# A graph-attention stage whose queries leave the first stage: keys and values only, edge features between the tiles, biases folded

## The chip, the cores and the metric

The kernel runs on one core of a Trainium2 chip. The metric is device time in microseconds, from the program's start to its end, less being better. The engines are TensorE (PE, and PEld for its weight loads), VectorE (DVE), ScalarE (ACT), GpSimd (POOL) and SyncE (SP), which only issues DMAs here.

## The reference

One graph attention layer and one expert layer over N = 6250 nodes of width D = 256, with E = 200000 edges sorted by their target `dst`, 4 heads of 64.

```
h   = layernorm(x)
enh = h + 0.1 * query_emb
Q, K, V = enh @ Wq + bq, enh @ Wk + bk, enh @ Wv + bv      # 4 heads of 64
mod_k  = K[src] + 0.2 * rel_w[edge_type]
scores = sum(Q[dst] * mod_k, -1) / 8
w   = softmax of scores over the edges of one dst
msgs = sum of w * V[src] per dst, or V where a node has no edge
x   = x + layernorm(msgs @ Wo + bo + h) * gamma + beta
x   = x + top-2 of 8 experts (256 -> 1024 gelu -> 256) on layernorm(x)
```

## The kernel before

The program is a sequence of blocks; each block holds one program per engine, and a block ends when all its engines and awaited DMAs have ended. They are: a load of the constants (`build`, L1740), `prepare`, `edge_pass`, a spare pass for unusual inputs that isn't entered, `after_edges`, and `experts`.

`prepare` is the first stage (L521 to L897). Its setup loads the weights and biases (SyncE, L607 to L626) and the edge lists (GpSimd, L649 to L687). VectorE alone makes the edge features from them (L739 to L798), each operation waiting for the one before through `link`. These are `feat` (for each edge, which of 16 rows of a window of nodes it belongs to, and its type), `bases` (the windows' first nodes), a check for unusual inputs, and the lists `keys`, `reach`, `delta` and `penc`. Only then does a loop over NT = 49 tiles of 128 nodes begin. `pipeline` runs every engine's `step`, and `T(k)` is the tile k steps behind. Per tile:

- SyncE loads x into `p_x` (L635), and stores `kept` (x + beta and h + bo, L640) and `kv` (keys and values, L642) of the tile five steps behind. There are R = 4 buffers. x of a tile is issued behind the stores of the tile six before it.
- VectorE takes mean and variance (L805, L819), the reciprocal of the root (L809), normalizes (L824), adds 0.1 query (L832), and evicts keys (L816), values (L827) and queries (L836) from PSUM with their biases.
- ScalarE takes the root (L713) and copies the transposed `enh` (L717) and the transposed queries into `QT` (L720), an SBUF tensor of all 6250 columns.
- TensorE transposes `enh` (L869), multiplies by `wkv` into one bank of 512 columns (L883) and by `wq` (L886), and transposes the queries (L876).
- GpSimd makes `kept` with two sums (L699, L701).

All matmuls are float32, and the trace shows two records for each of them. Last, the 13 tiles of the source lists `ends` are transposed into `idxall` (L841 to L845, L896).

`edge_pass` goes over 261 groups of 6 x 128 edges. GpSimd gathers keys and values of the sources (L240, six per group, U = 6 buffers); it waits for `s_agg`, the end of the sums of the group six before. TensorE's step transposes keys of group g+1 (L432), scores group g (L448 to L456) and sums group g-1 (L467). ScalarE copies `idx` and the window's queries `qb` out of `QT`. VectorE fills some constants at the front of this pass and signals `s_init`.

`after_edges` loads `Wo` and others first (L1215), normalizes and routes; `experts` computes the experts.

Of the kernel before, what the change touches and what calls it, by code (L numbers as in the profile page):

```python
# [8 lines left out]
ACT = mybir.ActivationFunctionType  # L9
# [7 lines left out]
P = 128  # L17
N, D = 6250, 256
H, HD = 4, 64
DC = D // P  # L20
# [117 lines left out]
def edge_pass(nc, ctx, cst, QT, kv_dram, idxall, feat_dram, accs_dram, bases, delta, penc, relT, reach, keys, spots):  # L138
# [60 lines left out]
    s_px = sem("es_px")  # L199

# [6 lines left out]
    with nc.Block() as blk:  # L207
# [39 lines left out]
        def _(act):  # L247
            act.preload_act_table(ACT.Exp)
            act.wait_ge(s_init, 4)

            def step(T):
                n = T(-AHEAD)
                if n.live:

                    if n.first >= U:
                        act.wait_ge(s_kv[n.slot], n.rnd * (16 * TG))
                    act.copy(idx[n.slot][:, :].rearrange("p (c j) -> p c j", c=2),
                             idxall[:, 0:2 * NG * TS].rearrange("p (c q) -> p c q", c=2)[:, :, bass.ds(n.t * TS, TS)]
                             ).then_inc(s_idx, 1)
# [160 lines left out]
        def _(pe):  # L420
            pe.wait_ge(s_init, 4)
# [99 lines left out]
def prepare(nc, ctx, cst, io, out, dram, QT, idxall, bases, delta, penc, relT, unfit, reach, keys):  # L521
# [9 lines left out]
    R = 4  # L531
# [3 lines left out]
    enh = [sb(f"p_enh{i}", [P, D]) for i in range(R)]  # L535
    enhT = [sb(f"p_enhT{i}", [P, DC, P]) for i in range(R)]
    qrow = [sb(f"p_q{i}", [P, D]) for i in range(R)]
# [3 lines left out]
    wq = sb("p_wq", [P, DC, D])  # L541
    bias = sb("p_bias", [P, 5, D])
    qe = sb("p_qe", [P, D])
    qe01 = sb("p_qe01", [P, D])
# [14 lines left out]
    odd = sb("p_odd", [1, 4])  # L559
# [7 lines left out]
    psT = ctx.enter_context(nc.psum_tensor("p_psT", [P, 512], F32))  # L567
    psKV = [ctx.enter_context(nc.psum_tensor(f"p_psKV{i}", [P, 512], F32)) for i in range(2)]
    psQ = [ctx.enter_context(nc.psum_tensor(f"p_psQ{i}", [P, 512], F32)) for i in range(2)]
    psQT = ctx.enter_context(nc.psum_tensor("p_psQT", [P, 512], F32))  # L570
    psI = ctx.enter_context(nc.psum_tensor("p_psI", [P, 2, 512], F32))
    ident = cst("ident")

    s_w = sem("ps_w")
# [13 lines left out]
    s_bn = sem("ps_bn")  # L588
    s_ln = sem("ps_ln")
    s_xb = sem("ps_xb")  # L590
    s_sd = sem("ps_sd")
    s_eT = sem("ps_eT")
    s_qT = sem("ps_qT")
    s_ev = sem("ps_ev")
    s_t = sem("ps_t")
    s_mm = sem("ps_mm")
    s_tq = sem("ps_tq")

    MF = 2 * len(chunks)
    SET0 = 8  # L600
    SET1 = SET0 + 14 * len(chunks) + 7
    SET2 = SET1 + 18
    rowof = [0, NG * TS, 2 * NG * TS]

    with nc.Block() as blk:
        @blk.sync
        def _(sp):  # L607
            for a in range(DC):
                rowsl = slice(a * P, (a + 1) * P)
                sp.dma_start(wkv[:, a, 0:D], io["Wk"][rowsl, :]).then_inc(s_w, 16)  # L610
                sp.dma_start(wkv[:, a, D:2 * D], io["Wv"][rowsl, :]).then_inc(s_w, 16)
                sp.dma_start(wq[:, a, :], io["Wq"][rowsl, :]).then_inc(s_w, 16)
            for j, name in enumerate(("bq", "bk", "bv", "bo", "beta")):
                sp.dma_start(bias[:, j, :], io[name].rearrange("(a d) -> a d", a=1).to_broadcast([P, D])
                             ).then_inc(s_w, 16)
            sp.dma_start(qe[:, :], io["query"].rearrange("(a d) -> a d", a=1).to_broadcast([P, D])
                         ).then_inc(s_w, 16)
# [10 lines left out]
            def step(T):  # L628
                g = T(0)
                if g.live:  # L630
                    r0 = node_rows(g.t)
                    if g.first >= R:
                        hold(sp, s_ln, (g.t - R) * 3 + 2)
                        hold(sp, s_xb, (g.t - R) * 2 + 1)
                    sp.dma_start(xin[g.slot][:, :], io["x"][bass.ds(r0, P), :]).then_inc(s_x[g.slot], 16)  # L635
                o = T(5)
                if o.live:
                    lo, r = own_rows(o.t)
                    hold(sp, s_xb, o.t * 2 + 2)
                    sp.dma_start(dram["kept"][r, :], kept[o.slot][lo:P, :]).then_inc(s_st[o.slot], 16)  # L640
                    hold(sp, s_ev, o.t * 3 + 3)
                    sp.dma_start(dram["kv"][r, :], kvrow[o.slot][lo:P, :]).then_inc(s_st[o.slot], 16)  # L642
            pipeline(sp, NT, 0, 5, R, 2 * R, step)
# [6 lines left out]
        def _(pool):  # L650
# [6 lines left out]
            pool.dma_start(seq[0:GE, 0:E // GE], io["dst"].rearrange("(p e) -> p e", p=GE)).then_inc(s_seq, 16)  # L657
# [30 lines left out]
            for c, (g0, n) in enumerate(chunks):  # L688

                pool.wait_ge(s_set, SET0 + 14 * (c + 1))  # L690
                for a in range(2):
                    pool.dma_start(dram["feat"][a, g0:g0 + n], feat[c][0:n, a]).then_inc(s_f, 16)

            def step(T):
                g = T(0)
                pool.wait_ge(s_x[g.slot], (g.rnd + 1) * 16)
                if g.first >= R:
                    pool.wait_ge(s_st[g.slot], g.rnd * 32)
                pool.tensor_tensor(kept[g.slot][:, D:2 * D], xin[g.slot][:, :], bias[:, 4, :], ALU.add).then_inc(s_xb, 1)  # L699
                pool.wait_ge(s_ln, g.t * 3 + 2)  # L700
                pool.tensor_tensor(kept[g.slot][:, 0:D], xn[g.slot][:, :], bias[:, 3, :], ALU.add).then_inc(s_xb, 1)  # L701
            pool.wait_ge(s_w, 16 * 18)
            pipeline(pool, NT, 0, 0, R, R, step)

        @blk.scalar
        def _(act):
            act.preload_act_table(ACT.Sqrt)

            def step(T):
                g, e, q = T(0), T(2), T(5)  # L710
                if g.live:
                    act.wait_ge(s_bn, g.t * 2 + 2)
                    act.activation(stat[g.slot][:, 8:9], stat[g.slot][:, 7:8], ACT.Sqrt, bias=cst("eps")  # L713
                                   ).then_inc(s_sd, 1)
                if e.live:
                    act.wait_ge(s_t, e.t + 1)
                    act.copy(enhT[e.slot][:, :, :].rearrange("p a q -> p (a q)"), psT[:, 0:D]).then_inc(s_eT, 1)  # L717
                if q.live:
                    act.wait_ge(s_tq, q.t + 1)
# [1072 lines left out]
```

## Time and profile before

| what | us |
|---|---|
| time, median of 3 runs | 3416.37 (3415.4 to 3417.13) |
| the profiled execution | 3421.45 |
| its span, first to last instruction | 3419.6 |
| TensorE busy in the span | 2775.5 (81%) |
| GpSimd busy | 2020.8 (59%) |
| VectorE busy | 1676.3 (49%) |
| ScalarE busy | 1281.9 (37%) |

Shares of the whole span average over stages with different limits: the table is to be read beside the stages, whose borders in the trace are 231.9 (end of `prepare`), about 2238 (end of `edge_pass`) and about 2742 (`experts` begins).

### The profile page before, as it was taken

How to read it: one execution, taken by the hardware profiler on the slowest of the kernel's cores; microseconds unless marked ns; L12 is line 12 of the kernel's file. 1: busy time of each engine (PE TensorE's matmuls, PEld its weight loads, DVE VectorE, ACT ScalarE, POOL GpSimd, SP SyncE). 2: the span in 40 equal slices, each digit the busy share in tenths (PEclk: the TensorE clock that was granted, in tenths of full speed). 3: DMA queues.
4: the chain of work that ended last, by engine and by line, in shares of the span. 5: the costliest groups of instructions: out<-in, count | busy, mean ns of one | idle time of the engine just before them, and what ended most of it. 6: DMA issues, size and time to landing. Idle time of an engine off the chain costs nothing. (4 is left out here: it accounts for less than half of the span.)

```text
span 3419.6 us, 74395 instructions
## 1 busy us (share of the span) xinstructions
PE 2775.5 (81%) x19652; PEld 1892.4 (55%) x19652; DVE 1676.3 (49%) x6055; ACT 1281.9 (37%) x4194; POOL 2020.8 (59%) x2106
## 2 busy tenths in 40 slices
PE   2977878887788878888888878866555999999998
PEld 1644444444444444444444444544444888888887
DVE  5756555555555555555555555577671111111111
ACT  0224444444444444444444444423342222222222
POOL 3547777777777777777777777667762222222222
PEclk9989999999999899999999999955557999999999
DMA  4658888888888888888888888755436666666664
GB/s 112 215 192 237 240 244 244 237 243 244 243 240 243 242 244 241 240 243 244 239 241 244 244 242 236 227 162 155 151 123 207 185 184 184 184 184 184 184 184 101
DMA packets 337412, 721.17 MB, mean 211 GB/s; under 512 B 43947, under 2 KB 184226, under 8 KB 337217
## 3 DMA queue, kind: packets, MB, share of 16 engines
q0 software_dynamic: 152560, 456.14, 48.4%
q1 hardware_dynamic: 184784, 264.35, 24.9%
q14 instruction: 52, 0.42, 0.0%
q8 instruction: 16, 0.26, 0.0%
HBM read 639.58 MB, written 80.74 MB: 211 GB/s over the span
## 5 line engine op out<-in xcount | busy, mean ns | idle before, releaser
L240 POOL DMA_INDIRECT e_kv<-d_kv,e_idx x1566 | 1503.8, 960 | 496.8 <-issue 451.7
L432 PE MATMUL psK<-consts,e_kv 128*128 128x128 f32 x3132 | 545.6, 301 | 234.7 <-DMA e_kv<-d_kv,e_idx 233.9
L432 PEld LDWEIGHTS psK<-consts,e_kv 128*128 128x128 f32 x3132 | 354.5, 148 | 378.8 <-issue 319.4
L1615 POOL DMA_INDIRECT out<-f_y,f_whose x112 | 174.0, 1553 | 648.5 <-DVE f_y L1668 634.7
L1634 ACT ACTIVATE f_hT<-f_psH,f_b 128x256 f32<-128x256 f32 x448 | 212.5, 474 | 590.1 <-PE f_psH L1712 590.0
L1712 PE MATMUL f_psH<-f_xT,f_w 128*128 128x256 f32 x1792 | 398.2, 381 | 1.4 <-DVE f_xT L1654 1.4
L1702 PE MATMUL f_psY<-f_w,f_hT 128*128 128x256 f32 x1792 | 396.0, 379 | 0.0
L326 DVE COPY e_kT<-psK 128x384 f32<-128x384 f32 x522 | 287.8, 551 | 198.6 <-PE psK L432 197.5
L1712 PEld LDWEIGHTS f_psH<-f_xT,f_w 128*128 128x128 f32 x1792 | 342.0, 191 | 48.6 <-DMA f_w<-in_W 1.7
L1702 PEld LDWEIGHTS f_psY<-f_w,f_hT 128*128 128x128 f32 x1792 | 336.2, 190 | 43.4
L268 ACT COPY e_qb<-QT 64x32 f32 x1044 | 229.4, 220 | 307.8 <-issue 288.5
L467 PE MATMUL psA<-e_kv,e_probT 128*32 128x128 f32 x6264 | 337.9, 289 | 0.4 <-ACT e_probT L306 0.4
L285 ACT ACTIVATE e_carried<-psA,e_small 128x130 f32<-128x130 f32 x261 | 96.7, 370 | 622.3 <-PE psA L467 622.3
L363 DVE TENSOR_TENSOR e_accs<-psA,e_carried 128x128 f32<-128x128 f32 x261 | 76.4, 293 | 474.1 <-ACT e_carried L285 474.1
L274 ACT COPY e_kT<-psK 128x384 f32<-128x384 f32 x522 | 248.7, 476 | 130.2 <-PE psK L432 124.7
L456 PE MATMUL psD<-e_kT,e_qb 128*32 128x384 f32 x2088 | 253.4, 561 | 0.0
L505 PE MATMUL psP<-consts,e_prob 128*128 128x128 f32 x783 | 142.8, 291 | 123.3 <-ACT e_prob L294 123.3
L1654 DVE TENSOR_SCALAR f_xT<-f_psT,f_ln 128x256 f32<-128x256 f32 x112 | 55.8, 540 | 378.3 <-PE f_psT L1690 378.3
L351 DVE TENSOR_REDUCE e_small<-psD 128x1 f32<-128x384 f32 x261 | 145.0, 556 | 128.0 <-PE psD L456 124.6
L467 PEld LDWEIGHTS psA<-e_kv,e_probT 128*32 128x32 f32 x6264 | 124.9, 109 | 124.2 <-issue 95.5
L478 PEld LDWEIGHTS psA<-e_accs,e_carry 128*128 128x128 f32 x522 | 84.4, 203 | 190.5 <-issue 189.9
L1665 DVE TENSOR_TENSOR f_yb<-f_psY,f_b 128x256 f32<-128x256 f32 x112 | 47.6, 425 | 269.5 <-PE f_psY L1702 269.5
(238 smaller groups left out, 4176.2 us busy)
## 6 DMA issues: line engine op xcount, KB each, us to landing
f_w<-in_W SPq DMA_DIRECT2D x112, 1024.0 KB, 8.0
e_rows<-d_feat SPq DMA_DIRECT2D x174, 288.0 KB
e_kv<-d_kv,e_idx POOLq DMA_INDIRECT x1566
d_accs<-e_accs SPq DMA_DIRECT2D x87, 195.0 KB
f_xs<-d_xs SPq DMA_DIRECT2D x56, 258.0 KB, 2.8
n_kept<-d_kept SPq DMA_DIRECT2D x49, 256.0 KB, 3.4
d_kept<-p_kept SPq DMA_DIRECT2D x48, 256.0 KB, 2.2
d_kv<-p_kv SPq DMA_DIRECT2D x48, 256.0 KB, 2.0
```

What stands on the lines that cost most here:

```text
L240: pool.indirect_dma_start(out=kv[g.slot][:, t, :], out_offset=None, in_=kv_dram[:, :], in_offset=bass.IndirectOffsetOnAxis(ap=idx[g.slot][ ...
L268: act.copy(qb[a.slot % R][o * HD:(o + 1) * HD, :].rearrange("p (c b w o) -> p c b w o", c=2, b=DC, o=2)[:, c, :, :, o], QT[o * HD:(o + 1) ...
L274: act.copy(kT[a.slot % 2][:, 1, j * GH:(j + 1) * GH], psK[:, 1, 0:GH]).then_inc(s_kTa, 1)
L326: dve.tensor_copy(kT[a.slot % 2][:, 0, j * GH:(j + 1) * GH], psK[:, 0, 0:GH]).then_inc(s_kTv, 1)
L351: dve.tensor_reduce(sm[:, MX], psD[:, g.slot % 2, 0:GH], AX.X, ALU.max).then_inc(s_m, 1)
L432: mm = pe.transpose(psK[:, half, t * P:(t + 1) * P], kv[a.slot][:, third * TS + t, half * P:(half + 1) * P], ident)
L456: mm = pe.matmul(psD[own, g.slot % 2, 0:GH], qb[g.slot % R][:, own], kT[g.slot % 2][:, b, c * GH:(c + 1) * GH], start=False, stop=True, ti ...
L467: mm = pe.matmul(psA[own, 0:2 * HD], probT[c.slot % R][:, j, own], kv[c.slot][:, s * TS + j, D + b * P:D + (b + 1) * P], start=j == 0, sto ...
L1615: pool.indirect_dma_start(out=out[:, :], out_offset=bass.IndirectOffsetOnAxis(ap=whose[c.slot][:, a:a + 1], axis=0), in_=y[c.slot][:, a, : ...
L1634: act.activation(hT[:, c, :], psH[:, c % 4, 0:BT], ACT.Gelu, bias=b1[:, bass.ds(e * FC + c, 1)]).then_inc(s_g, 1)
L1702: mm = pe.matmul(psY[:, t, 0:D], hT[:, f, t * P:(t + 1) * P], w2[c.slot][:, f, :], start=f == 0, stop=f == FC - 1)
L1712: mm = pe.matmul(psH[:, f % 4, 0:BT], w1[g.slot][:, a, f * P:(f + 1) * P], xT[g.slot][:, a, :], start=a == 0, stop=a == DC - 1)
```

## The change

- The block that loads the constants goes; `prepare` loads them behind the first x tile and each engine waits for what it needs. R becomes 6. SyncE's order of loads is new: x 0, constants, Wk, Wv, x 1, query (by columns), bk, x 2 and 3, Wq, Wo, bv and bq (by columns), bo, beta, x 4 and 5, the relations, bases, mid, and the 781 KB of dst (`seq`, before on GpSimd). The last 13 of them are `SMALL`. `feat` is stored by SyncE at step 47 instead of by GpSimd.
- The tile's x is normalized by ScalarE (a scale and a bias per row) instead of VectorE. The sum with 0.1 query is gone: `0.1 query @ Wk + bk` is computed once as `biask` and added at the keys' eviction, `0.1 query @ Wv + bv` goes through Wo into `biaso` (the weights of a node's edges sum to 1), which takes bo's place in `kept`, and values are copied by ScalarE without a bias.
- TensorE multiplies keys and values alone, in two banks, and no queries. The transposed normalized x is copied straight into `QT`.
- The edge features are cut by `yield` into some 86 pieces, one or two of which VectorE does in each of 53 steps. All loops are written out instead of looped in hardware.
- `edge_pass` begins with the queries: 13 chunks of 512 columns, computed in place from `QT`, evicted by ScalarE with the bias `bqc`. ScalarE copies the first six `idx` ahead of them.
- `Wo` stays in SBUF from `prepare` to `after_edges`.

```
 # edge_pass
+            for t in range(U):
+                listed(t, t)
+
+            for i, q in enumerate(QCH):
+                act.wait_ge(s_q, i + 1)
+                for b in range(DC):
+                    act.activation(QT[:, b, q], psQ[i % 2][:, b, 0:q.stop - q.start], ACT.Identity,
+                                   bias=bqc[:, b:b + 1]).then_inc(s_qe, 1)
+            act.wait_ge(s_qe, DC * len(QCH))
             act.wait_ge(s_init, 4)
...
         @blk.tensor
         def _(pe):
+            for i, q in enumerate(QCH):
+                if i >= 2:
+                    pe.wait_ge(s_qe, DC * (i - 1))
+                for b in range(DC):
+                    for a in range(DC):
+                        mm = pe.matmul(psQ[i % 2][:, b, 0:q.stop - q.start], wq[:, a, b * P:(b + 1) * P], QT[:, a, q],
+                                       start=a == 0, stop=a == DC - 1)
+                mm.then_inc(s_q, 1)
+            pe.wait_ge(s_qe, DC * len(QCH))
             pe.wait_ge(s_init, 4)
...
 # prepare, SyncE
+            for s in range(R, NT + 5):
+                if s < NT:
+                    hold(sp, s_xn, s - R + 1)
+                    hold(sp, s_k1, s - R + 1)
+                    load(s)
+                if s == NT - 2:
+
+                    hold(sp, s_set, N_FEAT)
+                    for c, (g0, n) in enumerate(chunks):
+                        for a in range(2):
+                            sp.dma_start(dram["feat"][a, g0:g0 + n], feat[c][0:n, a]).then_inc(s_f, 16)
+                for o in (range(s - 4) if s == R else (s - 5,)):
+                    lo, r = own_rows(o)
+                    hold(sp, s_evv, o + 1)
+                    hold(sp, s_ek, o + 1)
+                    sp.dma_start(dram["kv"][r, :], kvrow[o % R][lo:P, :]).then_inc(s_st[o % R], 16)
+                    hold(sp, s_k0, o + 1)
+                    sp.dma_start(dram["kept"][r, :], kept[o % R][lo:P, :]).then_inc(s_st[o % R], 16)
...
 # prepare, GpSimd
+            pool.wait_ge(s_w, SMALL)
+            for g in range(NT):
+                i = g % R
+                pool.wait_ge(s_x[i], (g // R + 1) * 16)
+                if g >= R:
+                    pool.wait_ge(s_st[i], (g // R) * 32)
+                pool.tensor_tensor(kept[i][:, D:2 * D], xin[i][:, :], rowsof[:, BETA, :], ALU.add).then_inc(s_k1, 1)
+                if g == 0:
+                    pool.wait_ge(s_set, N_BO)
+                pool.wait_ge(s_xn, g + 1)
+                pool.tensor_tensor(kept[i][:, 0:D], xn[i][:, :], biaso[:, :], ALU.add).then_inc(s_k0, 1)
...
 # prepare, ScalarE
+            for s in range(NT + 4):
+                g, f, m, c = s, s - 1, s - 2, s - 4
+                if 0 <= m < NT:
+                    act.wait_ge(s_t, m + 1)
...
+                    act.copy(QT[:, :, bass.ds(node_rows(m), P)],
+                             psT[m % 2][:, 0:D].rearrange("p (a q) -> p a q", a=DC)).then_inc(s_eT, 1)
+                if 0 <= c < NT:
+                    act.wait_ge(s_mm, c + 1)
...
+                    act.copy(kvrow[c % R][:, D:2 * D], psKV[1][c % 2][:, 0:D]).then_inc(s_evv, 1)
+                if 0 <= f < NT:
...
+                    act.activation(xn[f % R][:, :], xin[f % R][:, :], ACT.Identity, bias=stat[f % R][:, 10:11],
+                                   scale=stat[f % R][:, 9:10]).then_inc(s_xn, 1)
+                if g < NT:
+                    act.wait_ge(s_bn, g * 2 + 2)
+                    act.activation(stat[g % R][:, 8:9], stat[g % R][:, 7:8], ACT.Sqrt, bias=cst("eps")
                                    ).then_inc(s_sd, 1)
...
 # prepare, VectorE
+            extra = setup()
+            for s in range(NT + 4):
+                g, f, c = s, s - 1, s - 4
...
+                    dve.bn_stats(stat[g % R][:, 0:6], xin[g % R][:, :]).then_inc(s_bn, 1)
+                if 0 <= f < NT:
+                    dve.wait_ge(s_sd, f + 1)
+                    dve.reciprocal(stat[f % R][:, 9:10], stat[f % R][:, 8:9]).then_inc(s_ln, 1)
+                if g < NT:
+                    hold(dve, s_bn, g * 2 + 1)
+                    dve.bn_aggr(stat[g % R][:, 6:8], stat[g % R][:, 0:6]).then_inc(s_bn, 1)
+                if 0 <= f < NT:
+                    dve.wait_ge(s_ln, f * 2 + 1)
+                    dve.tensor_scalar(stat[f % R][:, 10:11], stat[f % R][:, 6:7], stat[f % R][:, 9:10], -1.0,
+                                      ALU.mult, ALU.mult).then_inc(s_ln, 1)
+                next(extra, None)
+                if 0 <= c < NT:
+                    dve.wait_ge(s_mm, c + 1)
+                    if c >= R:
+                        dve.wait_ge(s_st[c % R], (c // R) * 32)
+                    dve.tensor_tensor(kvrow[c % R][:, 0:D], psKV[0][c % 2][:, 0:D], biask[:, :], ALU.add
+                                      ).then_inc(s_ek, 1)
+                    next(extra, None)
...
 # prepare, TensorE: step s transposes tile s - 2 and multiplies tile s - 3
+            for s in range(2, NT + 3):
+                m, k = s - 2, s - 3
+                if s == AT_COLS:
+                    pe.wait_ge(s_w, SMALL)
...
+                if 0 <= k < NT:
+                    pe.wait_ge(s_eT, k + 1)
...
+                    for j in range(2):
+                        mm = into(psKV[j][k % 2][:, 0:D], lambda a: QT[:, a, bass.ds(node_rows(k), P)],
+                                  lambda a: wkv[:, a, j * D:(j + 1) * D])
                     mm.then_inc(s_mm, 1)
```

The small products of TensorE stand at its steps 3 (`AT_COLS`), 6 (`AT_BO`), 30, 32 and, for the index lists, 36 to 42.

## Rows read from the trace of the kernel before

**Rows 1.** Windows: stretch, length, busy PE, PEld, DVE, ACT, POOL, granted clock, DMA share, GB/s

```profile
0.00:30.30 30.30, 0.00 (x0) 0.00 (x0) 0.54 (x4) 1.30 (x2) 14.45 (x30) 1.00 0.87 218
30.30:65.90 35.60, 2.77 (x8) 1.53 (x8) 30.42 (x75) 0.00 (x0) 3.90 (x7) 1.00 0.06 23
65.90:221.90 156.00, 151.20 (x586) 94.58 (x586) 117.96 (x393) 40.79 (x146) 75.67 (x97) 1.00 0.57 200
221.90:231.90 10.00, 2.46 (x15) 1.61 (x15) 3.16 (x6) 0.38 (x1) 0.00 (x0) 0.84 0.11 42
```

**Rows 2.** Line L240, GpSimd's gathers: ns min/median/max, first and last start

```profile
L240 POOL DMA_INDIRECT e_kv<-d_kv,e_idx x1566: 949/953/1483, 234.5 to 2214.4; - x196
```

**Rows 3.** Timeline, two steps of the edge pass, TensorE: start, us, what

```profile
279.86 0.85 PE L432 MATMUL psK<-consts,e_kv 128*128 128x128 f32 x6
...
284.15 0.43 PE L467 MATMUL psA<-e_kv,e_probT 128*32 128x128 f32 x8
...
286.14 0.85 PE L432 MATMUL psK<-consts,e_kv 128*128 128x128 f32 x6
```

**Rows 4.** Timeline, TensorE in one tile of the first stage

```profile
142.38 0.38 PE L869 MATMUL p_psT<-consts,p_enh 128*128 128x128 f32 x2
...
142.81 1.88 PE L883 MATMUL p_psKV<-p_wkv,p_enhT 128*128 128x512 f32 x4
144.53 1.03 PE L886 MATMUL p_psQ<-p_wq,p_enhT 128*128 128x256 f32 x4
145.40 0.38 PE L869 MATMUL p_psT<-consts,p_enh 128*128 128x128 f32 x2
```

**Rows 5.** Waits between 80 and 210: total us, times, longest

```profile
DVE p_stat L805 <- DMA p_x<-in_x: 14.0, 22, 2.3
DVE p_kv L816 <- PE p_psQ L886: 13.1, 29, 0.8
```

**Rows 6.** Timeline, SyncE at the start

```profile
0.72 0.40 SPq L1740 DMA_DIRECT2D consts<-in_consts  x1
4.37 0.34 SPq L610 DMA_DIRECT2D p_wkv<-in_Wk  x1
```

**Rows 7.** Timeline, first tiles, VectorE and TensorE

```profile
69.82 0.42 DVE L805 BATCH_NORM_STATS2 p_stat<-p_x 128x6 f32<-128x256 f32 x1
...
70.44 3.62 PE L883 MATMUL p_psKV<-p_wkv,p_enhT 128*128 128x512 f32 x4
70.44 0.88 DVE L824 TENSOR_SCALAR p_xn<-p_x,p_stat 128x256 f32<-128x256 f32 x1
```

**Rows 8.** Timeline, first tiles, SyncE and VectorE

```profile
77.81 0.34 SPq L642 DMA_DIRECT2D d_kv<-p_kv  x1
...
78.30 0.34 SPq L635 DMA_DIRECT2D p_x<-in_x  x1
...
80.62 0.43 DVE L805 BATCH_NORM_STATS2 p_stat<-p_x 128x6 f32<-128x256 f32 x1 [0.51 <-DMA p_x<-in_x]
```

**Rows 9.** Timeline of a steady tile, VectorE, then SyncE

```profile
142.06 0.43 DVE L805 BATCH_NORM_STATS2 p_stat<-p_x 128x6 f32<-128x256 f32 x1 [0.68 <-DMA p_x<-in_x]
...
143.97 0.42 DVE L836 TENSOR_TENSOR p_q<-p_psQ,p_bias 128x256 f32<-128x256 f32 x1
...
147.77 0.43 DVE L805 BATCH_NORM_STATS2 p_stat<-p_x 128x6 f32<-128x256 f32 x1 [0.35 <-DMA p_x<-in_x]
...
144.52 0.33 SPq L642 DMA_DIRECT2D d_kv<-p_kv  x1
145.67 0.35 SPq L635 DMA_DIRECT2D p_x<-in_x  x1
```

**Rows 10.** Timeline, VectorE in the setup

```profile
55.36 1.83 DVE L781 TENSOR_TENSOR p_drop<-p_seq 125x1600 f32<-125x1600 int32 x1
```

**Rows 11.** Timeline, SyncE at the end of the stage

```profile
222.02 0.24 SPq L642 DMA_DIRECT2D d_kv<-p_kv  x1
```

**Rows 12.** Tile p_enh, VectorE: ns min/median/max

```profile
L832 DVE TENSOR_TENSOR p_enh<-p_xn,p_qe x49: 409/417/946, 67.6 to 213.0; 128x256 f32<-128x256 f32 x49
```

More of the change, by code:

```diff
@@ L199, in edge_pass @@
     s_px = sem("es_px")
+    s_q = sem("es_q")
+    s_qe = sem("es_qe")
+    QCH = [slice(q, min(q + 512, N)) for q in range(0, N, 512)]
+    psQ = (psD, psK)
     LO, HI, WARM = -1, 2, 8
@@ L252, in step @@
                 n = T(-AHEAD)
[L253 to L259, printed above, removed]
+                if n.live and n.first >= U:
+                    act.wait_ge(s_kv[n.slot], n.rnd * (16 * TG))
+                    listed(n.t, n.slot)
                 a = T(-1)
@@ L518, in own_rows, with prepare @@
     return lo, bass.ds(node_rows(t) + lo, P - lo)
[L521 removed]
+def prepare(nc, ctx, cst, io, out, dram, QT, idxall, bases, delta, penc, relT, unfit, reach, keys, wq, wo, bqc, consts):
     def sb(name, shape, dt=F32):
@@ L626, in _ @@
                                                                                ).to_broadcast([P, 1])).then_inc(s_w, 16)
[L628 to L643, printed above, removed]
+            sp.dma_start(seq[0:GE, 0:E // GE], io["dst"].rearrange("(p e) -> p e", p=GE)).then_inc(s_w, 16)
+            for s in range(R, NT + 5):
[15 more added lines that the diff above has]
+                    sp.dma_start(dram["kept"][r, :], kept[o % R][lo:P, :]).then_inc(s_st[o % R], 16)
             for i in range(R):
@@ L838, in _, with broadcast @@
-            pipeline(dve, NT, 0, 4, R, 2 * R, step)
-            dve.wait_ge(s_src, 16 * 5)
-            dve.tensor_copy(endsf[:, :, :], ends[:, :, :]).then_inc(s_back, 1)
-            for i, c in enumerate(range(0, IT, 4)):
-                n = min(IT - c, 4)
-                dve.wait_ge(s_turn, i + 1)
-                dve.tensor_copy(idxall[:, c * P:(c + n) * P], psI[:, i % 2, 0:n * P]).then_inc(s_back, 1)
+            def broadcast(which, col):
+                for a in range(DC):
+                    link(dve.tensor_scalar(spread[:, which, a, :], cst("ones"), cols[:, col, a:a + 1], None, ALU.mult))
@@ L847, in _ @@
+            for _ in extra:
+                pass
         @blk.tensor
         def _(pe):
-            pe.wait_ge(s_w, 16 * 18)
-            for b in range(2):
-                mm = pe.transpose(psQT[:, b * NREL:(b + 1) * NREL], relraw[:, :], ident[0:NREL, 0:NREL])
-            mm.then_inc(s_pb, 1)
-            pe.wait_ge(s_set, SET1)
-            for a, ps in enumerate((psT, psKV[1])):
-                pe.matmul(ps[:, 0:NG], cst("ones")[0:1, :], basef[0:1, a, :], start=True, stop=True).then_inc(s_pb, 1)
@@ L857, in _, with into @@
-            pe.wait_ge(s_set, SET1 + 4)
-            pe.matmul(psKV[0][0:1, 0:1], misfits[:, 0:1], cst("ones")[:, 0:1], start=True, stop=True
-                      ).then_inc(s_pb, 1)
-            pe.wait_ge(s_set, SET1 + 14)
-            def step(T):
-                g, m, c = T(2), T(3), T(5)
-                if g.live:
-                    pe.wait_ge(s_ln, g.t * 3 + 3)
-                    if g.first >= 1:
-                        pe.wait_ge(s_eT, g.t)
+            def into(ps, lhs, rhs):
+                for a in range(DC):
+                    mm = pe.matmul(ps, lhs(a), rhs(a), start=a == 0, stop=a == DC - 1)
+                return mm
```

427 lines of the change are left out of this document (235 added, 192 removed).

## The prediction

> **What bounds the kernel now.** I read the table of stages first [rows 1]. The whole first stage ends at 231.9; the edge pass runs from there to about 2215 and the rest needs no more than a glance, since the change leaves it as it is. In the edge pass GpSimd's gathers are the bound: 1566 of them start between 234.5 and 2214.4, one per 1.265 us, six per group, 7.59 us per group [rows 2]. TensorE needs less: a step with all its data present takes 286.14 - 279.86 = 6.28 us [rows 3]. So a microsecond saved before 231.9 is kept in full, provided that the gathers are not held up later.
>
> Before 231.9 there are four stretches [rows 1]. To 30.3 the engines wait for the first loads. From 30.3 to 65.9 VectorE computes the edge features alone (30.4 us busy in 35.6) and TensorE does nearly nothing. From 65.9 to 221.9 come the 49 node tiles. From 221.9 to 231.9 almost nothing computes.
>
> In the tile stretch TensorE is full: a tile is 3.02 us from transpose to transpose, of which the key/value matmuls take 144.53 - 142.81 = 1.72, the query ones 145.40 - 144.53 = 0.87, and two pairs of transposes 142.81 - 142.38 = 0.43 [rows 4]. The waits show a second bound just under it: VectorE waited 14.0 us for x tiles and 13.1 for TensorE [rows 5]. The reader should keep that in mind: the load of tile o+6 is behind the stores of tile o in SyncE's program, and x arrives late 22 times already.
>
> **The change, part by part.**
>
> *Start.* The block that waited for the constants goes. SyncE's first ordinary load was issued at 4.37 after a start at 0.72, and the wait for all 18 loads ended at 30.3 with the DMA queues full (share 0.87 of the stretch) [rows 1, 6]. The new kernel must still have almost the same bytes before its second tile: four broadcast vectors of 128 KB go, Wo (256 KB), two more x tiles (256 KB) and the 4-byte column loads come, and the 781 KB copy of dst moves to the end of SyncE's queue, which `SMALL` waits for. TensorE waits for `SMALL` ahead of tile 1, GpSimd ahead of its first tile. I take 30.3 - 3.7 for the earlier start, + 3 for bytes and small packets now in front: 29.5, bounds 26 and 33.
>
> *Fill.* Behind that wait TensorE has 8 one-column products and then slow matmuls: the first four key/value records took 3.62 us instead of 1.88 [rows 4, 7]. Tile 0 is done at about 36, tiles 1 and 2 at 38 and 40, then the small products for `biaso`, GpSimd's first sum at 42.5 and the next at 44. `kept` of tiles 0 and 1 must be issued before x of tile 7, so VectorE's step 7 starts at about 44.6 + 2.3 = 47.
>
> *A tile.* TensorE loses the queries and one pair of transposes: 3.02 - 0.87 - 0.22 = 1.93 us. Moving keys and values into separate matmuls of 256 columns costs nothing by the query ones, whose four records of that width take 0.87. ScalarE has a copy of 0.37, one of 0.35, the new normalization (about 0.38, the size of VectorE's) and a root of 0.29: 1.4 us, no bound. GpSimd's two sums stay at 1.6. What binds is the loop through SyncE: key eviction of tile o ends; SyncE issues kv(o), kept(o), x(o+6), 0.49 apart [rows 8]; x arrives 80.62 - 78.30 = 2.3 after its issue [rows 8], and I take 2.5 because 512 KB of stores now stand right ahead of it; then VectorE goes from bn_stats to the operation behind bn_aggr in 0.62 [rows 7], does the small product (0.1 to its issue), one piece of edge work, and evicts the keys of tile o+2, 0.42 for a tile of this form [rows 9]. That is two tiles per 0.1 + 0.98 + 2.5 + 1.14 = 4.7 us plus the piece: 2.3 to 2.4 us a tile bare, 2.55 with a piece of 0.5. The same sum for the old order: from the end of the eviction (143.97 + 0.42) to the kv store 0.13, to the load 145.67 - 144.52 = 1.15, to bn_stats 147.77 - 145.67 = 2.1, through VectorE's old step 143.97 + 0.42 - 142.06 = 2.33 [rows 9]: 5.7, or 2.85 a tile. That is just under TensorE's 3.02, as the waits had it [rows 5], so the loop is real.
>
> *Edge features.* Their work is 30.4 us of the setup [rows 1], plus the index turning (2.2, and a cast of 1.0), plus about 3 for the folded biases. Counting the generator's pieces against the steps, steps 7 to 26 hold about 1.0 us each. VectorE's own chain is 1.14 with the eviction, so 2.2, which fits under 2.55. Steps 27 to 30 hold 2.0, 2.4, 2.6 and 2.9 (the 1.83 us comparison over dst [rows 10], the reduction of the same size, the cast of the lists, the scan): with 1.14 each, 14 us. Steps 31 to 48 have little: 18 x 2.3 = 41.4. Steps 49 to 52 load nothing: 4 x 1.93 = 7.7. The six `feat` stores, formerly issued by GpSimd in idle time, now stand in SyncE's program ahead of the last tiles: 2.5 us of issue and 0.8 MB of queue, 3 us. The four index turnings add 1.5. Sum: 47 + 20 x 2.55 + 14 + 41.4 + 7.7 + 4.5 = 165.6.
>
> *Tail.* Before, the last `kv` store was issued at 222.02 [rows 11] and the stage let go at 231.9, while DMA was busy at a share of 0.11 and moved 42 GB/s [rows 1]: the two last stores, of 106 partitions and 212 KB each, crawl. Both stay, now issued together, so 10.7 us where it was 9.9. Stage end: 176.5, against 231.9: **55.4 earlier**.
>
> *Queries in the edge pass.* TensorE now computes 13 chunks of 4 matmuls before its first group. Per column that is what a tile's queries cost: 0.87 x 6250/128 = 42.5 us, plus about 2.5 for a start at the low clock (the granted clock is down to 0.84 over the stretch ahead [rows 1], and low it costs 3.62 against 1.88 for the same records [rows 4, 7]) and for the last eviction: 45. The evictions, 26 on ScalarE of about 0.6, hide under it. Then come a filling step of 3.7, one without sums of 4.9, and the sums of group 0 at 284.15 + 0.43 - 279.86 = 4.7 into the third step [rows 3]: 13.3. Group 0 is done 58.3 after the stage boundary. GpSimd has six buffers: it starts 2.6 in (234.5 against 231.9) and has issued 36 gathers at 2.6 + 45.5 = 48.1 [rows 2]. It then stands until 58.3: **10.2 us lost**, once. The backlog goes away because a step of 6.28 beats 7.59. What is queued behind GpSimd's wait is only further gathers. Moving the index copies ahead of `s_init` gives 0.3 back.
>
> *Wo's loads* leave the third stage. GpSimd's gathers bound the beginning there as well: I count nothing, and it could only add to the gain.
>
> **Sum.** -55.4 + 10.2 - 0.3 = -45.5. The profiled execution took 3421.45 us (span 3419.6, 1.9 around it), which is 5.1 above the median of 3416.37. I put the difference on the median: 3371.
>
> **A rule weighed.** The edge work now runs beside GpSimd's sums. One VectorE operation with two SBUF inputs already varies from 0.409 to 0.946 us beside them, with a median of 0.417 [rows 12]. The Trainium skill, page "SBUF — State Buffer", section "SBUF: two separate sides", says that VectorE (in its two-port modes, or with two SBUF inputs) and GpSimd take a shared port pair exclusively, for a whole instruction. The trace agrees for this operation; nothing here shows it for the integer casts. By the spread of the row, 0.946 - 0.417 = 0.5 for an operation that meets a sum: nothing if the pieces fall between the sums, as the median has it, 20 steps x 2 pieces x 0.5 = 20 us if all meet one. I count nothing in the sum, since 2.2 has 0.35 of slack under 2.55; the other end is rival 2.
>
> **Rivals.**
> 1. *TensorE binds after all* (x arrives in time, because chains of different parity overlap or the queue is quick): steps of 1.93 after the edge work, 2.2 (VectorE) within it. 47 + 44 + 14 + 35 + 8 + 3 = 151, stage end 162, -70 + 10 = -60: 3356. For it: VectorE waited for x only 22 of 43 times [rows 5]. Against it: the loop sum, which comes out at 2.85 where the waits show it near 3.02. Chance 0.17.
> 2. *VectorE binds* through the port and x comes later still behind the stores, 3.0 us in the first twenty steps and 2.7 after: +9 +7, and with pieces that meet GpSimd in steps 27 to 30, +3: about -26: 3390. Chance 0.20.
> 3. *The gathers lose far more than 10 us*: if a backlogged step took 7.6 instead of 6.28, the backlog would never shrink, but the loss would stay at what is lost at first; if on top TensorE stayed at its low clock (records of twice the length [rows 4, 7]) through all the queries, group 0 is done at 87 + 13 + 8 = 108 and 60 us are lost: -55 + 60 = +5: 3421. It turns slower once the queries take over 90 us. Against it: in the tile stretch the long records of the beginning [rows 7] had become the short ones [rows 4] with nothing but matmuls back to back, and the queries are just that. Chance 0.03.
> 4. *The change gives nearly nothing early*: the loads in front, with 4-byte columns, reach beyond 45 us. Chance 0.03, about 3390 at the worst, which the range takes in.
>
> **Chances and range.** Forecast (3371, its own range 3362 to 3382) 0.57, the rivals as above. The range 3353 to 3395 reaches over rivals 1 and 2. A measurement of this kernel tells about 0.2%, 7 us, from no change: faster 0.95, same 0.02, slower 0.03.
>
> **What would show it.** Right: p_x still the wait ahead of bn_stats, a tile of 2.3 to 2.6 us with TensorE idle 0.4 or more in each; the stage boundary near 176; one wait of GpSimd for psA of about 10 us and then none; 42 to 46 us of query matmuls. A boundary near 162 shows rival 1; tiles of 3 us with VectorE busy throughout, rival 2; matmul records of double length all through the queries, rival 3. The prediction is wrong if steps with edge work leave VectorE without idle time, or if GpSimd waits for psA in many groups.

## The result, and the profile after

The changed kernel takes 3378.0 us (median of 4 runs, 3376.1 to 3380.7), the kernel before 3415.9 beside it: ratio 0.989, 95% interval 0.987 to 0.991, so 37.9 us less. The forecast was 3371, within 3353 to 3395. The profiled execution took 3379.7 us, against 3421.45 before.

The table of stages of the changed kernel (columns as in [rows 1]):

```profile
30.10:48.10 18.00, 17.04 (x72) 14.09 (x72) 5.11 (x25) 5.78 (x17) 5.53 (x9) 1.00 0.23 85
48.10:172.50 124.40, 100.45 (x457) 76.38 (x457) 81.88 (x290) 61.39 (x173) 66.59 (x91) 0.97 0.72 240
172.50:184.60 12.10, 0.00 (x0) 0.00 (x0) 0.00 (x0) 0.00 (x0) 0.00 (x0) 0.57 0.20 71
```

TensorE, with 151.2 busy in 156 us the bound of the tile stretch before [rows 1], now stands idle for 24 of 124 us. The stage lets go at 184.6, where it was 231.9: 47.3 us earlier.

Timeline of the changed kernel, VectorE in two consecutive steps, then SyncE's loads and stores of the same time (idle before and releaser in brackets):

```profile
55.86 0.43 DVE L921 BATCH_NORM_STATS2 p_stat<-p_x 128x6 f32<-128x256 f32 x1
...
56.98 0.42 DVE L937 TENSOR_TENSOR p_kv<-p_psK,p_biask 128x256 f32<-128x256 f32 x1
57.32 0.35 DVE L856 CAST p_feat<-p_type 128x384 bf16<-128x384 int32 x1
60.52 0.43 DVE L921 BATCH_NORM_STATS2 p_stat<-p_x 128x6 f32<-128x256 f32 x1 [2.86 <-issue]
```

```profile
55.45 0.33 SPq L686 DMA_DIRECT2D d_kv<-p_kv  x1
55.91 0.35 SPq L688 DMA_DIRECT2D d_kept<-p_kept  x1
56.43 1.87 SPq L639 DMA_DIRECT2D p_x<-in_x  x1
58.88 0.34 SPq L686 DMA_DIRECT2D d_kv<-p_kv  x1
```

The order kv, kept, x is the loop of the prediction: a load is issued about 1 us behind the eviction that the kv store waits for, and VectorE's step two tiles later waits for its landing. Here one load took 1.87 us to issue instead of 0.34, and VectorE stood for 2.86. Between 48 and 172.5 VectorE stood three times for such a load (issues of 1.87, 0.87 and 1.69; 7.0 us together) and 15 times, 21.1 us, for x otherwise.

The waits between 48 and 172.5 of the changed kernel (total us, times, longest); the second row answers to the first of [rows 5]:

```profile
ACT p_xn L767 <- DVE p_stat L930: 39.6, 33, 3.2
DVE p_stat L921 <- DMA p_x<-in_x: 21.1, 15, 3.4
DVE p_stat L921 <- issue: 7.0, 3, 2.9
```

Behind the boundary, the gathers of the changed kernel, as [rows 2], and then GpSimd's waits between 150 and 260:

```profile
L244 POOL DMA_INDIRECT e_kv<-d_kv,e_idx x1566: 949/953/1467, 187.0 to 2179.4; - x196
```

```profile
POOL e_kv L244 <- ACT e_idx L254: 19.5, 1, 19.5
...
POOL e_kv L244 <- PE psA L491: 12.4, 1, 12.4
```

The gathers start 47.5 us earlier and end 35.0 earlier. What lies between is the one stall of 12.4 us for the sums of group 0; every later wait for them is 0.3. The first gather of the next stage (`n_agg`) starts 34.0 earlier, 2204.3 against 2238.3, and the end of the span comes 41.7 earlier. So 7.7 us more were gained behind the gathers, in code whose only edit is that Wo is no longer loaded there.

### The profile page after: what moved, and what is told of

Same layout as the page of the kernel before. It is cut to its first block and busy times, and to the rows that moved or that the text cites. A ratio compares the mean times of both kernels' runs of the same rounds, so it can differ in the third digit from the quotient of the medians.

```text
span 3377.9 us, 73501 instructions
## 1 busy us (share of the span) xinstructions
PE 2780.7 (82%) x19682; PEld 1902.6 (56%) x19682; DVE 1612.8 (48%) x5916; ACT 1327.4 (39%) x4269; POOL 2014.1 (60%) x2099
## 5 line engine op out<-in xcount | busy, mean ns | idle before, releaser
L529 PEld LDWEIGHTS psP<-consts,e_prob 128*128 128x128 f32 x783 | 80.8, 140 | 176.3 <-ACT e_prob L309 176.3
```

The costliest lines, as they stand in the source:

```text
L529: mm = pe.transpose(psP[:, j * P:(j + 1) * P], prob[g.slot % R][:, j * P:(j + 1) * P], ident)
```

## The experiments

All are made from the changed kernel, where nothing else is said. The boundary is where the query matmuls start (L441). The kernel before was run again beside each group of runs, with medians of 3415.9 to 3419.3 (3415.9 beside the changed kernel, 3419.0 beside the first four runs below), so a difference between two groups is uncertain by some 3 us; ratios are to the kernel before in the same group. Positions within a run come from one profiled execution each, and they vary too: the last eviction ends at 172.5, 175.0, 172.1 and 172.2 in the changed kernel and in the next three whose tiles are the same (stores split, one chunk, features by GpSimd).

**Stores a step later.** The loop's own test: the load of tile s is issued ahead of the stores of tile s-6 instead of s-5.

```diff
-            for s in range(R, NT + 5):
+            for s in range(R, NT + 6):
-                for o in (range(s - 4) if s == R else (s - 5,)):
+                for o in (s - 6,):
```

> Change: SyncE queues a tile's two stores one step later, so that the load of tile s goes ahead of the stores of tile s-6 instead of s-5; nothing else. Theory (the loop of x behind the stores, with the landing of x and the eviction of an older tile in it, sets the period of about 2.4 us): the load no longer waits on the previous tile's eviction, the normal period falls to what TensorE or VectorE need, 2.0 to 2.2 us, and the boundary after the first stage comes at 160 to 175 us instead of 184.6; total 3354 to 3369. Rival A (VectorE or TensorE is the bound, and the waits for x are only its shadow): period and boundary within 2 us of now, total 3376 to 3380. Rival B (the DMA engines, busy 0.72 here, are the bound): no change either, with the landing of x longer than 2.3 us.

Measured: 3358.5 us (3354.5 to 3359.4), 19.5 less than the changed kernel; ratio to before 0.9823 (0.9807 to 0.9839). The boundary comes at 163.8, 20.8 earlier. The loop now runs over three tiles instead of two, since a load waits for an eviction one tile older. Its stages, and its wait for x between 48 and 151.5:

```profile
48.10:151.50 103.40, 94.18 (x451) 73.71 (x449) 80.08 (x277) 59.20 (x169) 65.86 (x88) 1.00 0.84 283
151.50:163.80 12.30, 0.01 (x1) 0.04 (x1) 0.06 (x1) 0.05 (x2) 0.00 (x0) 0.62 0.21 73
```

```profile
DVE p_stat L921 <- DMA p_x<-in_x: 8.2, 8, 3.3
```

The same work is done in 103.4 us instead of 124.4, with TensorE busy 91% of it. Both rivals fall: neither TensorE nor VectorE nor the DMA engines (share 0.84 now, 0.72 then) were the bound. The place of two stores in SyncE's program was.

**The last stores split.** The last tile's two stores of 106 partitions become four, of 96 and 10 partitions.

```diff
+                    parts = [own_rows(o)] if o < NT - 1 else [
+                        (P - 96, bass.ds(N - 96, 96)), (NT * P - N, bass.ds(LAST + NT * P - N, N - (NT - 1) * P - 96))]
...
-                    sp.dma_start(dram["kv"][r, :], kvrow[o % R][lo:P, :]).then_inc(s_st[o % R], 16)
+                    for (lo, r), n in zip(parts, size):
+                        sp.dma_start(dram["kv"][r, :], kvrow[o % R][lo:lo + n, :]).then_inc(s_st[o % R], 16)
... (kept likewise; the wait at the end counts two stores more)
```

> Change: the last tile's two stores, of 106 partitions each, are made as 96 and 10 partitions each; nothing else. Theory (the 12.1 us between the last eviction and the boundary are the last stores landing slowly for their 106 partitions, 71 GB/s in that window against 240 before): the tail falls to 3 to 5 us, the total by 7 to 9 us to 3369 to 3371. Rival (the tail is the queue's remaining stores, or the end of the block itself): no change, 3376 to 3380.

Measured: 3370.3 us (3369.0 to 3372.4), 7.8 less; ratio 0.9855 (0.9839 to 0.9872). The last eviction ends at 175.0 and the boundary is at 179.0: a tail of 4.0 instead of 12.1. (The boundary is 5.6 earlier and not 8, since the tiles of this execution ended 2.5 later, with the same code.) The window of that tail:

```profile
175.00:179.00 4.00, 0.00 (x0) 0.00 (x0) 0.00 (x0) 0.00 (x0) 0.00 (x0) 0.72 0.64 219
```

In the changed kernel, of 40 slices between 165 and 186 the last stores' read

```profile
DMA  0898997000089999511111111111111111100005
GB/s 0 316 382 300 332 379 289 0 0 0 0 304 386 378 386 371 180 12 16 8 39 47 55 47 55 51 51 51 51 55 47 55 47 55 47 35 0 0 0 93
```

The stores crawl at mostly 47 to 55 GB/s, with between one and two tenths of the DMA engines busy; split, the same bytes move at 219 in the window above. The Trainium skill, page "DMA: Bandwidth & Descriptors", section "Why a DMA increments its semaphore by 16 and not by 1", says that a DMA uses the largest number of engines up to 16 that divides the outer dimension: 2 for 106, 16 for 96, 10 for 10. The trace agrees for 106 partitions (2 of 16 is 0.125). For the split stores it shows a share of 0.64 over the tail, far more than 2 engines, but not which store had how many.

**One chunk of queries.** The price of the moved queries; the run leaves out 12 of the 13 chunks.

```diff
-    QCH = [slice(q, min(q + 512, N)) for q in range(0, N, 512)]
+    QCH = [slice(q, min(q + 512, N)) for q in range(0, N, 512)][:1]
```

> Leaves out 12 of the 13 chunks of queries (the output is then not the reference's). Theory (the 45 us of queries lie beside the gathers' latency and the fill, and only the stall of GpSimd, 12.1 us by its longest wait, is on the path): the total falls by 11 to 14 us, to 3364 to 3367. Rival (the query work adds to the end in full, 41 us of the 45): the total falls to about 3337. Second rival (GpSimd's gathers catch up on their own): no fall.

Measured: 3366.6 us (3363.7 to 3367.8), 11.4 less, ratio 0.9844 (0.9827 to 0.9860), with the boundary at 184.4, as good as unmoved. GpSimd's wait for group 0's sums:

```profile
POOL e_kv L244 <- PE psA L491: 0.6, 2, 0.3
```

The 12 chunks left out are some 41 of the 44 us of query work; the time falls by about the stall of 12.4 alone.

**Edge features stored by GpSimd.**

```diff
-                            sp.dma_start(dram["feat"][a, g0:g0 + n], feat[c][0:n, a]).then_inc(s_f, 16)
+                if g == NT - 11:
+                    pool.wait_ge(s_set, N_FEAT)
+                    (the same six stores as pool.dma_start)
```

> Change: the six stores of edge features are issued by GpSimd after its tile 42 instead of by SyncE ahead of its stores of tile 46. Theory (they hold SyncE and the DMA engines while tile 48's load waits: a wait of 3.4 us at 160 us): boundary 2 to 4 us earlier, total 3374 to 3376. Rival (the last tiles wait for the stores ahead of them in any case, or GpSimd's issuing stalls kept rows): no change or 1 to 3 us slower.

Measured: 3377.0 us (3375.9 to 3380.1), ratio 0.9878 (0.9861 to 0.9894), boundary 184.5. That is 1.0 us less than the changed kernel, or 3.8 by the ratios, whose intervals overlap; that isn't separated from no change. In the profile the last load of x is issued at 160.4 instead of 161.2 and the last eviction starts 0.3 earlier (171.8 against 172.1). So the profile shows 0.1 to 0.7 us for the six stores on SyncE, where the prediction had 3, and the expected 2 to 4 us did not come; the times can't exclude them.

**The kernel before with stores a step later.**

```diff
-                o = T(5)
+                o = T(6)
... (the loop runs one step longer)
```

> The kernel before with the one edit of the run that moved the stores a step later: SyncE queues the stores of tile s-6 at step s instead of s-5. Theory (before, TensorE with 2.97 us a tile in steady state sets the pace, and the loop of load behind stores came into being with the change): no measurable change, ratio 0.998 to 1.002. Rival (the loop held the kernel before as well): 10 to 20 us faster. Its profile also says how far the stages after the first differ between two profiled executions of the kernel before: from the first n_agg to the end it took 1181.3 us; if that was the run, 1173 to 1177 now; if the change made those stages shorter, 1181 again.

Measured: ratio 1.0001 (0.9992 to 1.0010), 10 runs against 15. The edit that is worth 19.5 us in the changed kernel is worth nothing in the one before. Its trace says why. Between 80 and 210 VectorE no longer waits for x at all (14.0 us before, [rows 5]), and waits for TensorE instead, which is busy in 130.0 of the 130 us (129.5 before):

```profile
DVE p_kv L816 <- PE p_psQ L886: 29.7, 43, 1.1
```

Its profile also says what the two kernels differ in behind the gathers. From first `n_agg` to the end it took 1178.9 us, which lies in neither of the ranges expected. With the profiles of all runs of this section the picture is clear all the same: 1178.7 to 1181.6 in the four of before and its variants, 1171.7 to 1174.3 in the ten of the changed kernel and those made from it. Some 2.5 us vary from run to run; the rest, 4 us or more, is a property of the programs.

**Both edge pieces behind the eviction.**

```diff
-                next(extra, None)
+                if c < 0:
+                    next(extra, None)
                 if 0 <= c < NT:
                     ...
                                       ).then_inc(s_ek, 1)
                     next(extra, None)
+                    next(extra, None)
```

> The changed kernel, with both edge pieces of a step on VectorE behind the eviction of the keys (as it is, one lies between a tile's statistics and the eviction, one behind it). Same work, same stores. Theory (the loop runs from an eviction over SyncE and the load of x to the statistics and the next eviction but one; a piece ahead of the eviction lies in it, a piece behind it lies in the wait for x): with 0.3 to 0.4 us a piece, 0.15 to 0.2 us less per tile over some 40 tiles, total 4 to 8 us less, 3370 to 3374. Rival (VectorE's sum of work sets the period, wherever it stands in the step): no change, 3376 to 3380.

Measured: 3372.5 us (3369.8 to 3376.7), 5.5 less, ratio 0.9872 (0.9857 to 0.9887), whose interval overlaps the changed kernel's (0.9872 to 0.9907), so the time alone doesn't show a gain. The boundary tells more: 178.7, 5.9 earlier, where the same tiles varied by 3 in the four profiles named above. VectorE does the same work, but the piece now lies in the wait for x. Between 48 and 166.5 that wait, against 21.1 us and 15 times in the changed kernel, is

```profile
DVE p_stat L921 <- DMA p_x<-in_x: 27.1, 23, 3.5
```

VectorE waits longer and the kernel is faster. Its load isn't the bound; its order was a part of the loop.

**Both edits that paid.**

> The changed kernel with both edits that paid: stores a step later (measured -19.6 us alone) and the last tile's stores split into 96 and 10 partitions (-7.8 alone). Theory (one acts on the tiles, the other on the tail, so they add): 3349 to 3352. Rival (with the tiles closer together the last stores queue at the DMA engines, busy 0.85, and the tail grows again): 3354 to 3358.

Measured: 3349.6 us (3348.0 to 3352.0), ratio 0.9801 (0.9787 to 0.9814); last eviction 152.5, boundary 156.5, tail 4.0. They add: 19.5 + 7.8 = 27.3 expected, 28.4 measured, with the 3 us of uncertainty between groups.

**And the edge pieces behind the eviction as well.**

> As the run before, and with both edge pieces behind the eviction. Theory (with the stores a step later the load of x no longer waits for the eviction, TensorE is busy 94% of the steady stretch and sets the period, so where the pieces stand no longer matters): within 2 us of the run before. Rival (VectorE's order still sets the period): 3 to 6 us faster than it.

Measured: 3351.3 us (3344.5 to 3352.2), ratio 0.9799 (0.9786 to 0.9813). The boundary is at 154.1, 2.4 earlier, but the time is the same within the spread. In the profiles the gathers start 2.5 earlier, the stall for the sums of group 0 is 13.8 instead of 12.4, and the last gather starts only 0.3 earlier. Of the 5.5 us nothing that can be measured is left once the load waits for an eviction one tile older.

**The gap at VectorE's loop turn, three runs.** They ran on another chip, on which the kernel before takes 4006 us and the gathers end some 570 us later (below); the stage in question lasts as long there as before. The first two are the kernel before with

```diff
+            for _ in range(64):      # 24 in the second
+                dve.nop(nofuse=True)
```

> The kernel before with 64 instructions that do nothing on VectorE, at its start, where it waits for its loads until 40 us. Question: in the stage behind the gathers VectorE stands idle with nothing shown as its cause, before tile 26, 33 and 40 of 49 (where its loop of seven tiles turns), 21.2 and 19.6 us in two profiles of the kernel before and 11.7 to 13.9 us in all eight profiles of kernels made from the changed one. Theory (the gap depends on where the loop's code lies in VectorE's program, which the change moved): with the code moved by 64 instructions the gaps change, to 10 to 30 us, and the stage from first n_agg to first f_psT, 363.3 to 364.8 us before, with them; total 3410 to 3425. Rival (something the change did there, its one edit being that Wo is no longer loaded in it): 19 to 22 us and 363 to 365 us as they were.

> The same with 24 such instructions. Theory (place of the code): gaps of VectorE at the turn of the loop other than 19 to 22 us in this run or in the one with 64. Rival (Wo's loads, or data): 19 to 22 us in both.

> The changed kernel with Wo's two loads issued again at the start of the stage behind the gathers, and waited for there, as in the kernel before; nothing else. Theory (place of VectorE's code): gaps of VectorE at the loop's turns stay at 11 to 14 us, the stage from the first n_agg to the first f_psT at 356 to 357 us or up to 1 us more for the loads; total 3376 to 3380. Rival (those loads are what made the stage 7 us longer in the kernel before): 362 to 365 us, total 3383 to 3387.

Measured: ratios to before 1.0000 (0.9990 to 1.0010), 1.0002 (0.9992 to 1.0012) and 0.9913 (0.9897 to 0.9930). VectorE's idle time with no cause shown, in front of `n_y`: first the two profiled executions of before and after on the first chips, then 64 instructions more, 24 more, and the changed kernel with Wo's loads back:

```profile
DVE n_y L1364 <- issue: 21.2, 5, 7.0
```

```profile
DVE n_y L1469 <- issue: 13.0, 8, 4.1
```

```profile
DVE n_y L1366 <- issue: 21.1, 5, 6.9
```

```profile
DVE n_y L1366 <- issue: 19.3, 5, 6.6
```

```profile
DVE n_y L1470 <- issue: 13.0, 8, 4.3
```

The stage from first `n_agg` to first `f_psT` took 364.9, 362.9 and 357.5 us, against 364.8 and 356.6 in the two kernels. The loads of Wo account for 0.9 us of the 8.2 at most (357.5 against 356.6), and moving VectorE's code by 24 or 64 instructions left the gaps as they were. Neither theory explains the gap; the last section has what the traces show beside it.

**A chunk of queries in the tail.** From the kernel with both edits that paid: nodes 0 to 511 are projected behind the last tile, in the PSUM tiles of the transposes.

```diff
-    QCH = [slice(q, min(q + 512, N)) for q in range(0, N, 512)]
+    QCH = [slice(q, min(q + 512, N)) for q in range(512, N, 512)]
+            pe.wait_ge(s_eT, NT)
+            for b in range(DC):
+                mm = into(psT[b][:, 0:512], lambda a: wq[:, a, b * P:(b + 1) * P], lambda a: QT[:, a, 0:512])
+            mm.then_inc(s_mm, 1)
... (ScalarE evicts both halves into QT with bqc and waits for that)
```

> The kernel with stores a step later and the last stores split, and the first chunk of queries (nodes 0 to 511) made at the end of the first stage, behind the last tile's values, while the last stores land; 12 chunks stay beside the gathers. Theory (the tail of 4 us leaves TensorE idle, and the stall of GpSimd, 12 us, shrinks by what the queries end earlier): the chunk's 3.5 us are hidden in the tail, the boundary stays within 1 us, the stall falls by 3 to 4 us, total 3345 to 3347, ratio to before 0.979. Rival (the chunk, with its eviction, ends after the stores have landed and holds the boundary by what it saves): no change against the run without it, 3349.6, ratio 0.980.

Measured: 3346.7 us (3344.9 to 3351.3), ratio 0.9792 (0.9778 to 0.9805). The boundary is at 159.3, 4.7 behind the last eviction (154.6) where it was 4.0 (156.5 and 152.5). It is 2.8 later, not within 1 us as expected, 2.1 of it from tiles that the edit doesn't touch. The stall

```profile
POOL e_kv L244 <- PE psA L491: 7.3, 1, 7.3
```

was 12.4; it fell by 5.1, more than the expected 3 to 4. In the profile the gathers, first to last, take 1985.6 instead of 1992.3. By the medians it is 2.9 us faster than the run without it, with overlapping intervals: the stall is shorter, the gain of the whole isn't shown beyond the spread.

## Why the prediction was right

In the profiled executions the sum reads: boundary -47.3 (forecast -55.4), the first gather behind it -0.2 (forecast -0.3), gathers from first to last +12.5 (forecast +10.2 of stall), the step from the last gather to `n_agg` +1.0, behind it -7.7 (forecast 0). Together -41.7, forecast -45.5. By the medians it is -37.9, as measured beside the changed kernel, and with before's 3417.5 of the later 15 runs -39.5; before's profiled execution was slower than its median, as the prediction had it.

*Start and fill: right, within about 1 us.* TensorE came out of its wait at 30.1 (29.5), VectorE's step 7 started at 48.1 (47).

*The mechanism of the tile: right, and shown.* The experiment on the stores took the loop away and with it 21 us of the stage; the pieces moved behind the eviction took 5.9, close to half a piece a tile; and before, where TensorE's 3.02 lay above the loop's 2.85, the same edit did nothing. *Its size: too small.* The term that failed is the tile with edge work, 2.55: the 20 steps from 48.1 to 103.6 took 55.5 us, 2.77 each, 4.5 us more than forecast. 1.0 of that is a slip in the prediction's own working, since (4.7 + 0.5) / 2 is 2.6. What was left out are the slow issues of loads: three in these steps, 1.5, 0.5 and 1.4 us longer than 0.34. If they lie in the loop in full they make 3.4 us, the rest; no run removed them alone, so this share is worked out and not shown. TensorE's clock is no part of it: it was granted at 0.50 (1.2 GHz) from 62 to 65 and from 96 to 99, behind idle times of 2.49 and 2.16, as here,

```profile
58.51 1.03 PE L947 MATMUL p_psV<-p_wkv,QT 128*128 128x256 f32 x4
62.02 0.69 PE L994 MATMUL p_psT<-consts,p_xn 128*128 128x128 f32 x2 [2.49 <-ACT p_xn L767]
62.50 1.91 PE L947 MATMUL p_psK<-p_wkv,QT 128*128 128x256 f32 x4
```

but VectorE's eviction waited for TensorE in none of these steps, only for the last three tiles (5.2 us). ScalarE's normalization also takes 0.60, not the 0.38 taken from VectorE's, but lies in no loop that bound:

```profile
L767 ACT ACTIVATE p_xn<-p_x,p_stat x49: 599/600/612, 17.4 to 166.1; 128x256 f32<-128x256 f32 x49
```

Steps 27 to 30 took 13.8 (14), the rest 55.2 (53.6). The last eviction ended at 172.5, not 165.6. (With a tail of 10.7 the prediction's stage end is 176.3, not the 176.5 that it went on with.)

*The tail: 12.1, not 10.7*, and with the right cause, 106 partitions. *The queries: 44 (45), slow start included.* The granted clock was 0.50 (1.2 GHz) from 184.6 to 186, behind 12 us in which TensorE did nothing, and a record there took 1.19 us instead of 0.59. For the slow records of [rows 7], which the prediction put down to the same low clock, the trace doesn't show it: the granted clock reads 1.00 from 70 to 78. *The stall: 12.4, not 10.2*, since group 0 was done 59.8 behind the boundary, not 58.3, and the gathers were ready 0.6 sooner.

*Rival 1* (3356, boundary 162) is what the changed kernel becomes with the stores a step later: 163.8 and 3358. *Rival 2*, VectorE as the bound through the port (3390), is the nearest in time beside the forecast, since 3378 lies between the two, but not its mechanism: with the stores a step later the same VectorE work fits into 103 us instead of 124. The subtraction over the edges, with one SBUF tensor as input, stayed near its shortest time beside GpSimd's sums:

```profile
L842 DVE TENSOR_SCALAR p_epos<-p_epos,p_start x6: 768/785/869, 52.4 to 95.3; 128x384 f32<-128x384 f32 x4, 5x384 f32<-5x384 f32 x2
```

An operation with two SBUF inputs did meet a sum at 107.8. It was the sum that lasted longer there, 1.81 us instead of the usual 0.73, and not VectorE's operation (1.82; 1.83 in [rows 10]).

*Rivals 3 and 4* are out by the same rows: 44 us of queries, one stall of 12.4, and TensorE out of its wait at 30.1.

*Wo's loads* were counted at nothing. Putting them back cost at most 1 us, so that stands. The 7.7 us that the stage behind the gathers gained were foreseen by nothing, and they made good most of what the tiles lacked: the right total owes as much to that as to the sum. That part is luck. Without it the time would have been near 3386, still within 3353 to 3395 but outside the forecast's own 3362 to 3382, and nearer to rival 2's 3390 than to 3371.

## What to carry to other kernels

When one engine's work per tile is cut, write out the loop that runs through the queue of loads and stores, from an eviction over the store that waits for it and the load queued behind that store to the next tile but one: it can be the next bound, and one more step between a load and the stores ahead of it may stretch it out of the way (here half of what the change itself gave, and nothing in the kernel where TensorE was the bound). Look at the number of partitions of a stage's last stores: with 106 they took 12 us to land, as 96 and 10 they took 4. Work moved beside a latency still shows as far as it delays the first result for which a full set of buffers waits.

## What the runs showed of the hardware that was not expected

- *VectorE stands idle where its loop of seven tiles turns.* In the changed kernel, where the eviction of tile 26 is ready to go:

```profile
2361.60 0.18 DVE L1444 BATCH_NORM_AGGREGATE n_st<-n_st 128x2 f32<-128x6 f32 x1
2364.89 0.42 DVE L1469 TENSOR_TENSOR n_y<-n_psO,n_kept 128x256 f32<-128x256 f32 x1 [3.12 <-issue]
```

and in the kernel before, the same two instructions:

```profile
2395.02 0.18 DVE L1339 BATCH_NORM_AGGREGATE n_st<-n_st 128x2 f32<-128x6 f32 x1
2402.17 0.42 DVE L1364 TENSOR_TENSOR n_y<-n_psO,n_kept 128x256 f32<-128x256 f32 x1 [6.96 <-issue]
```

  In the profile a packet of 8 KB on the queue called instruction falls into these gaps, and into none of VectorE's other pauses of over 1.5 us in this loop. In the changed kernel, 2361.8 to 2364.8:

```profile
q14 instruction: 1, 0.01, 0.8%
```

  In the kernel before VectorE halts twice at each turn, with an instruction of its sequencer of 0.2 us between the halts, and each halt has its packet. From 2395.2 to 2398.9, then from 2399.1 to 2402.1:

```profile
q14 instruction: 1, 0.01, 1.2%
q14 instruction: 1, 0.01, 0.6%
```

  The loop's code is the same. The gaps sum to 11.7 to 13.9 us in all ten profiles of kernels made from the changed one, or of itself, and to 19.3 to 21.2 in the four of before and its variants, on each chip, and TensorE waits through them. All 14 profiles have the pattern above: at each of the three turns two halts of 2.2 to 3.8 us, each with one packet, in before and its variants, and one halt of 2.8 to 4.0 with one packet in the others. So VectorE seems to wait there for its own code, two pieces of it against one, which would give the 8 us. That is read from the traces and not shown by a run; why one program needs two pieces is open. The loads of Wo and a shift of the code by 24 or 64 instructions don't decide it; a larger shift was not tried.
- *A load's issue on SyncE sometimes takes 1.7 to 1.9 us instead of 0.34*, twice among the 40 loads issued between 50 and 165 of the changed kernel, with two more of 0.87 and 0.99. What makes them slow is open. With the stores a step later there was one of 2.04, and VectorE stood 1.0 us for it instead of 2.9.
- *One chip ran the edge pass more slowly.* Between 1000 and 2000 us its granted clock was 0.85, where the changed kernel had 0.92 on the first, and it moved 188 GB/s instead of 242; GpSimd, the bound of [rows 2], there waits for TensorE's sums:

```profile
1000.00:2000.00 1000.00, 789.90 (x5718) 468.65 (x5718) 435.55 (x1565) 359.39 (x1224) 586.87 (x613) 0.85 0.69 188
```

```profile
1000.00:2000.00 1000.00, 820.62 (x7383) 475.90 (x7383) 560.36 (x2018) 452.91 (x1579) 759.24 (x791) 0.92 0.85 242
```

  The first window is of the run with Wo's loads back, the second of the changed kernel. 613 gathers were issued in it instead of 791, and the kernel before takes 4006 us instead of 3416. The order of the two kernels holds there (ratio 0.991), but the bound of its longest stage is another, and why is open. That run also had its query matmuls last 66.7 us instead of 44, since ScalarE's evictions stood still once for 19.7 us and TensorE with them for 15.6, and GpSimd's longest wait for the sums was 35.4 instead of 12.4. What held ScalarE the trace doesn't say.
